# Zeros of the first layer's query and key tiles: set by two compute engines instead of transferred

## The reference, cut to what matters

```python
xn = layer_norm(x, norm_w, norm_b)
q = (xn @ q_w + q_b).reshape(B, T, H, -1)
k = (xn @ k_w + k_b).reshape(B, T, H, -1)
att = jnp.einsum('bnhl,bmhl->bnmh', q, k)
att = softmax(att + (1.0 - mask) * -1000000.0, axis=2)
v = ((xn @ v_w + v_b) * src_mask[:, :, None]).reshape(B, T, H, -1)
y = jnp.einsum('bnmh,bmhl->bnhl', att, v).reshape(B, T, D)
e = silu(emb) @ emb_w + emb_b
scale, shift = jnp.split(e[:, None, :], 2, axis=2)
h = silu(layer_norm(y, sb_norm_w, sb_norm_b) * (1.0 + scale) + shift) @ out_w + out_b
return x + h
```

## Time and profile before

| | |
|---|---|
| median of 3 executions | 897.27 us (896.86 to 898.52) |
| the profiled execution | 897.85 us |
| its span, first to last instruction | 895.9 us |
| PE busy, share of the span | 863.8 us, 96% |
| PEld | 718.4 us, 80% |
| DVE | 764.8 us, 85% |
| ACT | 669.7 us, 75% |
| POOL | 614.7 us, 69% |
| DMA, mean over the span | 121 GB/s |

### The profile page before, as it was taken

One profiled execution on the slowest core, in us unless ns is written; L12 is line 12 of the kernel. 1 busy time (PEld: TensorE's weight loads), 2 busy tenths in 40 slices (PEclk: granted clock), 3 DMA queues, 4 the chain that ended last, 5 costly groups with the idle time before them and its releaser, 6 DMA issues.

```text
span 895.9 us, 23756 instructions
## 1 busy us (share of the span) xinstructions
PE 863.8 (96%) x8432; PEld 718.4 (80%) x8432; DVE 764.8 (85%) x1577; ACT 669.7 (75%) x1200; POOL 614.7 (69%) x1095
## 2 busy tenths in 40 slices
PE   5899999999999999999999898999999999999996
PEld 4677777777777777777776567899999999999996
DVE  5789999999999999999998657788888888888876
ACT  2257777777777777677777777888888888888875
POOL 3456575756666665757574347888888888888875
PEclk9999999999999999999999999999999999999999
DMA  8862535343434434344433223123222222222111
GB/s 260 255 196 102 184 114 179 119 168 130 162 136 149 149 138 159 137 151 146 150 124 139 88 71 120 35 88 88 87 84 87 90 86 88 87 86 87 39 31 59
DMA packets 77412, 108.54 MB, mean 121 GB/s; under 512 B 7088, under 2 KB 43408, under 8 KB 77168
## 3 DMA queue, kind: packets, MB, share of 16 engines
q1 hardware_dynamic: 77296, 107.03, 35.5%
HBM read 35.60 MB, written 16.88 MB: 59 GB/s over the span
## 4 chain that ended last, share of the span: by engine, by line
PE 90%; DVE 3%; ACT 3%; issue 3%; POOL 1%; SPq 0%; DMA 0%; DVEq 0%; ACTq 0%; POOLq 0%
PE psX L1353 16%; PE psY L1468 13%; PE psM L1353 10%; PE psT L1353 9%; PE psT L1449 6%; PE psT L1430 5%; PE psY L1353 5%; PE psM L1449 3%; PE psT L1364 3%; PE psT L1633 3%; PE psY L1583 3%; PE psY L1489 3%; PE psM L1364 3%; PE psM L1430 2%; PE psX L1501 2%
## 5 line engine op out<-in xcount | busy, mean ns | idle before, releaser
L984 DVE TENSOR_REDUCE sb_cm<-psT 128x4 f32<-128x1024 f32 x168 | 202.5, 1216 | 12.3 <-PE psT L1449 12.1
L600 ACT ACTIVATE sb_P<-psT 128x1024 f32<-128x1024 f32 x176 | 177.7, 1026 | 30.0 <-PE psT L1430 14.5
L1468 PE MATMUL psY<-sb_P,sb_Vp 128*17 128x256 f32 x2048 | 129.2, 381 | 1.0 <-DVE sb_yr L1010 0.7
L984 DVE TENSOR_REDUCE sb_cm<-psM 128x4 f32<-128x1024 f32 x88 | 107.0, 1216 | 7.7 <-PE psM L1449 7.7
L404 POOL TENSOR_SCALAR sb_ve<-sb_mv 128x2 f32<-128x2 f32 x32 | 7.3, 229 | 134.4 <-DVE sb_mv L1018 134.3
L1353 PE MATMUL psX<-sb_xT,sb_W0h 128*128 128x256 f32 x488 | 93.7, 294 | 0.0
L600 ACT ACTIVATE sb_P<-psM 128x1024 f32<-128x1024 f32 x80 | 82.0, 1025 | 14.4 <-PE psM L1430 6.7
L1468 PEld LDWEIGHTS psY<-sb_P,sb_Vp 128*17 128x17 f32 x2048 | 50.6, 97 | 46.8 <-issue 6.1
L421 POOL TENSOR_TENSOR sb_qp<-sb_qp 128x512 fp32r<-128x512 f32 x64 | 82.1, 1282 | 5.3
L1449 PE MATMUL psT<-sb_Ks,sb_Qs 64*128 64x256 f32 x672 | 74.7, 305 | 3.2 <-DVE sb_cm L984 1.9
L1430 PE MATMUL psT<-sb_Qs,sb_Ks 64*128 64x256 f32 x704 | 74.5, 295 | 1.9 <-ACT sb_P L600 1.9
(11 more groups left out here) (206 smaller groups left out, 2583.5 us busy)
## 6 DMA issues: line engine op xcount, KB each, us to landing
sb_Qs<-sb_qp SPq DMA_DIRECT2D x96, 256.0 KB
sb_Ks<-sb_qp SPq DMA_DIRECT2D x96, 256.0 KB
sb_xt<-in_x SPq DMA_DIRECT2D x32, 256.0 KB, 3.0
y_normed<-sb_Yn SPq DMA_DIRECT2D x32, 256.0 KB, 2.0
sb_u<-in_x SPq DMA_DIRECT2D x32, 256.0 KB, 2.9
sb_u<-y_normed SPq DMA_DIRECT2D x32, 256.0 KB, 3.1
out<-sb_v SPq DMA_DIRECT2D x31, 256.0 KB, 2.2
sb_v<-key_mask SPq DMA_DIRECT2D x32, 128.0 KB, 3.5
```

The source lines that it names most:

```text
L600: a.activation(P[G % 4][:, :], pairs[place["S", n, g][0]][:, :], ACT.Exp).then_inc(s_ex, 1)
L984: v.tensor_reduce(cm[n % 2][:, 4 * j:4 * j + 4], scores, AX.X, ALU.max, negate=True).then_inc(s_mx, 1)
L1468: ins = pe.matmul(psY[32 * j:32 * j + 17, y0:y0 + T], Vp[n % RING][:, m, 4 * gr + j, :], Pj[:, c0:c0 + 256], start=(m == 0), stop=(m == 1))
```

## The change: what it does, and the diff

The zeros of a tile are now written by a compute engine: all of `Qs[0]` by DVE, as its first instruction, all of `Ks[0]` by POOL at its start, and both tiles of rings 1, 2 and 3 by POOL (`cleared(i)`): ring 1 after the small memsets that end the start, ring 2 in turn 1 and ring 3 in turn 2, in each between `vmask` and `xnorm`. `filled(i)` transfers four partitions for each tile, the rows of ones, in place of 32, after waits for the two new semaphores. So the rows of a transfer go from 256 KB to 32 KB. The number of transfers and their places stay.

```diff
@@ semaphores
+        p_qk, p_later = sem("p_qk"), sem("p_later")
@@ block.sync
             def filled(i):
 
-                for w, tile in enumerate((Qs[i], Ks[i])):
-                    sp.dma_start(tile[3:128:4, :, :], ones[:, w:w + 1, :].to_broadcast([32, 8, T])).then_inc(p_fill, 16)
+                sp.wait_ge(p_qk, 2)
+                if i >= 1:
+                    sp.wait_ge(p_later, 2 * i)
+                for w, (tile, at) in enumerate(((Qs[i], MASKS), (Ks[i], SHIFTS))):
+                    sp.dma_start(tile[at, :, :], ones[1 - w:32:8, w:w + 1, :].to_broadcast([4, 8, T]))\
+                        .then_inc(p_fill, 16)
@@ block.gpsimd
             g.wait_ge(p_pool, 2)
+            g.memset(Ks[0][:, :, :], 0.0).then_inc(p_qk, 1)
             xnorm(0)
             for i in range(RING):
                 ins = g.memset(Vp[i][:, :, :, 16:17], 1.0)
             ins.then_inc(p_pool, 1)
             g.wait_ge(p_pool, 3)
+
+            def cleared(i):
+                for tile in (Qs[i], Ks[i]):
+                    g.memset(tile[:, :, :], 0.0).then_inc(p_later, 1)
+
+            cleared(1)
+
@@ block.gpsimd, loop over turns
                 if ok(t - 1):
                     vmask(t - 1)
+                if 1 <= t < RING - 1:
+                    cleared(t + 1)
                 if ok(t + 1):
                     xnorm(t + 1)
@@ block.vector
+            v.memset(Qs[0][:, :, :], 0.0).then_inc(p_qk, 1)
             v.memset(psY[:, T:2 * T], 0.0).then_inc(p_zero, 1)
             stats(0, 0)
```

## The result

| | before | after |
|---|---|---|
| median | 897.56 us (4 executions, 896.86 to 898.52) | 903.20 us (4, 901.31 to 904.26) |
| the profiled execution, its span | 897.85, 895.9 | 904.26, 902.5 |
| ratio | | 1.0047, 95% interval 1.0028 to 1.0066 |

The change makes the kernel slower: by 5.6 us between the medians, by 4.2 us (2.5 to 5.9) by the ratio, which is an estimate of its own and not the quotient of the two medians. The direction and the place were right; the size was above the forecast of 3.1 us, and one of its causes was not in the prediction at all.

What follows compares the result with a forecast made beforehand. PE, busy 96% of the span and full from 60 us on, bounds the kernel, so earlier shifts reach the end. Terms +1.2 - 1.3 + 0 + 3.2 + 0 = +3.1 us on 897.3 give 900.4 us, range 898.0 to 902.8.

Steps and rivals of the forecast that it cites:

- The price of a memset on POOL: 128x2048 memset on POOL: 1.75 us each, 3.5 a pair (2.3 to 5.0); on DVE 2.2 us.
- DVE blocked by ring 1's pair: Start, `first_weight`: DVE stands still beside POOL's memsets, delaying the path to the first `rowmax`; +1.2 us (0 to 1.8).
- served between them: 0: Start: if DVE's weight instruction is served between POOL's two ring 1 memsets, DVE is late by 0.
- The keys' wait goes: Before the first `rowmax`: smaller transfers land the keys some 1.5 us earlier, removing PE's 1.30 us wait; -1.3 us.
- Ring 2's pair hidden: Turn 1: POOL is free for 3.96 us and the pair takes 3.5; 0, at most +0.5 us.
- Ring 3's pair, `xturn(3)` 2.4 us late: Turn 2: the pair delays `xnorm(3)` by 3.5 us against 1.1 us of slack; PE stands still for 2.4 us.
- The first `rowmax` of sequence 2 late by 3.2: Turn 2: late queries and keys, 3.5 us less 0.3 of slack; +3.2 us (1.7 to 5.0), including `xturn(3)`'s 2.4.
- short memsets: Rival: POOL memsets take 1.15 us each, so the sum is +1.0 us, 898.3 us; chance 0.17.
- the transfers decide: Rival: not slower; POOL has room in turn 2, smaller transfers bring -1.3 us, 896.0 us; chance 0.10.
- the scores' path has room: Rival: late keys of sequence 2 are absorbed, only `xturn(3)` counts; +2.3 us, 899.6 us; chance 0.14.
- the change doesn't do what it says: Rival: SP still waits for the fill, taking away the -1.3; 901.7 us, counted within the forecast's own range.
- Full blocking: Rival: both ring 1 memsets, 2.1 us each, hold DVE up 2.5 us; sum +5.1, 902.4 us; chance 0.14.

Runs made afterwards that it cites:

- both_moved: Changed kernel with ring 3's pair in turn 1 behind the splits and ring 1's `Qs[1]` memset on DVE before its weights wait: 896.43 us, ratio 0.9988.
- ring3_early: Changed kernel with ring 3's pair of memsets moved from turn 2 to turn 1, behind both splits: 897.77 us, ratio 1.0004.
- filler: Changed kernel with 20 unused matmuls on PE in its gap ahead of `xturn(3)`: 903.17 us, run again 902.04 us.
- second pair of profiles: Profiled executions of the repeat runs of the changed kernel (median 903.73 us) and of filler (902.04 us).
- ring3_behind_xnorm: Changed kernel with ring 3's pair in turn 2 placed behind `xnorm(3)`, ahead of the splits of sequence 2: 901.88 us, ratio 1.0054.
- run 8: Not a run label: in "when they run 8 us earlier" it is a verb and a time; the kernel meant there is ring3_early, 897.77 us.
- both_moved_full_transfers: As both_moved, but `filled` transfers the 32 partitions of the kernel before: 897.16 us, ratio 0.9995.

## Why the prediction was right or wrong, point by point

- **The price of a memset on POOL, 1.75 us a piece, 3.5 a pair:** right (3.55). DVE's was 1.76 in place of 2.2, hidden in either case.
- **DVE blocked by ring 1's pair, +1.2:** right in cause; that the number is near is partly luck. The pair of `sb_W0h` took 1.16 us longer in the profiled execution, but 0.9 to 2.0 in the six profiled executions with both memsets, and both_moved puts it at 1.5. In those six it ended between 11.76 and 11.97 us, wherever between 9.27 and 10.24 it had started, just behind the second memset, which ended between 11.36 and 11.81. In four of them the first instruction of the pair stood still until then; in two (ring3_early and filler) it was served between the memsets, and the second stood still for the whole second memset. So the prediction's "served between them: 0" was wrong: being served there gained nothing. With one memset ending at 9.8 the pair took 0.64. The two-port rule of the Trainium skill (SBUF — State Buffer, "Who interferes with whom") is borne out, and for a memset, which only writes. By it the term is 1.8 at a start of 9.71; the three profiles with a start between 9.59 and 9.84 show 1.5 to 1.7, and the changed kernel's 1.16 goes with a small load that happened to land later (10.18).
- **The keys' wait goes, -1.3:** it went, but -1.3 was too much. The transfers freed more than the 1.5 us that I took for ring 0: the large load behind them (`sb_EW`) landed 7.9 us after its issue in place of 12.1. Yet PE only got what DVE left it: alone, with DVE free, the smaller transfers are worth 0.8 us.
- **Ring 2's pair hidden, 0:** right. POOL was done at 28.14, and its next work came at 28.59, released by DVE.
- **Ring 3's pair, `xturn(3)` 2.4 us late:** right (2.46, idle 2.35).
- **The first `rowmax` of sequence 2 late by 3.2:** the mechanism was right, the size was not. By the late keys alone it is 3.8 (57.78 and 57.84 in the second pair of profiles), so the 0.3 us of room I took was not there for the full pair; ring3_early against the filler kernel, both at the full clock, gives 3.8 as well. In the profiled execution of the changed kernel it was 6.58.
- **The step that was missing:** the sum priced a gap of PE by its length and took the clock for 1.00, because the one profile of before showed 1.00 everywhere. The gap of 2.35 us was followed by low clock in both profiles of the changed kernel, and between the medians the loss was 5.6 us, where the schedule alone makes some 4 (filler at the full clock: 901.5 against 897.2). With the terms as measured the prediction's own sum would be 1.5 - 0.8 + 3.8 = 4.5 in place of 3.1. The same omission makes the kernel before look steadier than it is.
- **The rivals:** short memsets and "the transfers decide" fell with the 1.8 us rows; that the scores' path has room fell with ring3_behind_xnorm; that the change doesn't do what it says fell with the wait for the keys, which is gone. "Full blocking" was closest in time (902.4), but by luck: DVE was held until the second memset's end, as it says, at a price of 1.5 us and not 2.5, its memsets of 2.1 us took 1.8, and the lower clock was not in it.
- **The range:** the median of 903.2 lies 0.4 us above it; by the ratio, 897.3 x 1.0047 = 901.5, it lies within.

## What to carry to other kernels

Before work is put on an engine that looks idle, look at what stands behind it in that engine's own order: the same two memsets cost some 5.5 us ahead of a normalization (903.2 and 903.7 against 897.8), which are gone when they run 8 us earlier, behind the splits. A memset on GpSimd also stops a VectorE `tensor_scalar` between SBUF tiles, so the two want to be apart in time. And a gap of TensorE may cost more than its length where nothing hides the low clock behind it; look at several executions by their granted clock, since one profile may hide how often it is low.

## What the runs showed of the hardware that I had not expected

- The granted clock was at half (1.2 GHz) for stretches of a few us, in the profiles that had them all within the first 70 us. By the mean clock this befell about half of the executions of the kernel before (27 of 54 below 0.999) and all 10 of the changed one. In the kernel before, 0.002 less of the mean clock goes with 1.5 us more.
- A DVE memset of 2048 float32 elements in SBUF took 1.76 us, 0.86 ns an element, each time with a POOL memset under way beside it; that of 256 in PSUM took 0.27 us, 1.06 each. POOL's memset took 1.8 us beside DVE's and without it, so POOL was not slowed; no run shows a large DVE memset alone.
- The same small load (`sb_rb`), for which DVE waits before the weights, landed between 9.27 and 10.35 us in different executions.
- Two transfers of 256 KB within SBUF, to every fourth partition, cost the load behind them 4.2 us (12.1 against 7.9), more than twice what the mean rate of the stretch gives; between both_moved and both_moved_full_transfers, which differ in this alone, it was 3.3 us (11.2 against 7.9).
